# One attention and expert kernel: its projections issued as pairs of 64-column matmuls right behind P V, half of its score peaks copied out of PSUM by ScalarE, and its expert items in another order

## The chip, the cores and the metric

One core of one Trainium2 chip. The metric is the device time of one launch in microseconds (us), the median of several runs. The inputs are fixed, everything is float32.

## What is computed

A transformer block with adaptive layer norm, batch 1, 2048 tokens of width 128:

```python
mod = (silu(c) @ wmod)              # six vectors of 128: shift, scale, gate, twice
h = layernorm(x) * (1 + ca) + sa
x = x + ga * attention(h)           # 16 heads of 64
h = layernorm(x) * (1 + cb) + sb
x = x + gb * experts(h)             # 8 experts of 128, top 2 by sigmoid, and one shared expert
```

The attention reads its projections with a plain `reshape(1, 16, 2048, 64)` of the (2048, 1024) result. So head n uses tokens 128n to 128n+127 alone, and each of these tokens gives 16 "positions" of 64 values: 2048 positions per head. The scores are 2048 x 2048 per head, followed by softmax and P V. The expert part multiplies each token by the router's weight before and after an expert's SwiGLU, and sums over the chosen two; the shared expert has no weight.

## The kernel before

**Work.** The kernel goes through 16 heads; a head is two units (half 0 and half 1 of its queries), a unit is 16 key tiles (kt), and two key tiles are a step, so a unit has 8 steps and 32 places, numbered 4 x step + 0 to 3. On TensorE (PE) places 0 and 1 of a step are the scores of one key tile each (`scores`, L1149 to L1179), places 2 and 3 the product of probabilities and values of one key tile of the step before (`weigh`, L1182 to L1194). Scores are split into three products of float32r parts (hi x hi, hi x lo, lo x hi: L1166, L1169, L1172), each a pair of matmuls in two row tiles of the array (64 rows by 128 columns). `weigh` (L1190) is float32 in two column tiles (128 rows by 64 columns, `tile_position=(0, 0)` and `(0, 64)`).

**Peaks.** The softmax needs the largest score of each query ahead of time. A pair (`pair`, L1099 to L1115) is a rough product of 128 queries with 512 keys in each of two PSUM banks (6 and 7). VectorE (DVE) reduces it to its maximum (`pair`, L918 to L929, the reduction is L924). There are 16 pairs per unit, for the next unit or the one after. PE issues one at each place 1 and one at each place 3, and each waits until the banks of the one before are free (`peak_free`). After pair 15 the partial maxima are reduced to 8 per query (L928), PE transposes them (`turn_shift`, L1122), DVE keeps them and a DMA spreads them for the next unit's scores (L1178).

**Side jobs.** `side_jobs` (L80) lays out by hand at which place each job of a unit is issued: `LONG_JOBS` has the projections of the next head (q twice, k twice, v twice: `side`, L1082 to L1097), the output projection of the head before (`project`, L1207 to L1216) and the shift. `SUM_PLACES` has the sums over the probabilities (`sum_unit`, L1203), `SCALE_PLACES` the reciprocals in four parts (L944) and the scaling (L951), `LOW_PLACES` the low parts of q and k (L901, L907, L915). All these jobs go through PSUM bank 5 and wait for `job_free`. Within a place the order is that of the list: pairs first, then the long jobs. Every engine walks the same plan in its own program, so a job's place sets the order of work on PE, DVE, ScalarE (ACT) and on SP's DMA queue.

**Other engines.** ACT takes the exponentials, 128 x 1024 per key tile (L786), copies q, k and v out of PSUM (`side`, L705 to L715; k twice, L710 and L712), rounds the step of k (L720) and copies P V (L737). GpSimd (POOL) sums the probabilities, 15 adds of 128 x 1024 per unit (`add_tile`, L851). PE's sum of a unit waits for all 15 of them.

**Experts.** 36 items: 4 groups of 512 tokens, in each the shared expert and then the 8 experts (`ORDER`, L392). An item is two up products (L439, L440), SiLU on ACT (L481), products on DVE (L546, L548) and four down products (L425). The routed items need their tokens weighted first (`weigh_tokens`, L408, L413): items 1 and 2 (`FIRST_WEIGHED`) on DVE, all others on POOL, behind its last attention add. `SUM_AFTER` and the names beside it (L403 to L406) say behind which item the rest of the last head's work comes: its sum needs POOL's last add.

Of the kernel before, what the change touches and what calls it, by code (L numbers as in the profile page):

```python
# [11 lines left out]
P = 128  # L12
# [6 lines left out]
BANK = 512  # L19
# [31 lines left out]
    {6: ("inv", 0), 7: ("inv", 1), 9: ("inv", 2), 11: ("inv", 3), 13: ("scale", 0)},  # L51
    {10: ("inv", 0), 12: ("inv", 1), 15: ("inv", 2), 19: ("inv", 3), 21: ("scale", 0)},
# [27 lines left out]
def side_jobs(half, sums=True, project=True, pairs=True, early=True, last_head=False):  # L80

    places = [[] for _ in range(4 * PAIRS)]
    if sums:
        places[SUM_PLACES[half]].append(("sum", 0))
# [7 lines left out]
    for place, (kind, i) in LONG_JOBS[half].items():  # L92
        if sums if kind == "out" else pairs if kind == "shift" else project:
            places[place].append((kind, i))
# [12 lines left out]
def build(nc, x, wq, wk, wv, wo, gate_w, w1, w2, w3, sw1, sw2, sw3, expert_bias, cond, wmod, out):  # L107
    with ExitStack() as ctx:
# [53 lines left out]
        mod_t = sb("mod_t", [P, 4, 2])  # L162
        peak_parts = sb("peak_parts", [P, 2, PEAK_PAIRS // STRETCHES, STRETCHES])
        peak = sb("peak", [P, 8])
# [35 lines left out]
        peak_full, peak_free = sem("peak_full"), sem("peak_free")  # L200
        tail_full, tail_free = sem("tail_full"), sem("tail_free")
# [27 lines left out]
        class Tail:  # L229

            def __init__(self, n):
                self.n, self.full = n, n + 1
                self.bank = PEAK_BANK + n % 2 if n < TAIL_PAIRED else PV_BANK
                self.earlier = n - 1 if n < TAIL_PAIRED else n
                self.ps = ps[:, self.bank, :]

# [155 lines left out]
        ORDER = [EXPERTS] + list(range(EXPERTS))  # L392

        def routed(m):

            return m // ALL * EXPERTS + m % ALL - 1

        ITEMS = GROUPS * ALL

        FIRST_WEIGHED = (1, 2)  # L400
# [4 lines left out]
        GATE_AFTER = (13, 14, 15, 16)  # L405
        LATE_AFTER = {10: ("turn", 3), 12: ("logits", 1), 18: ("weights", 3)}  # L406

        def weigh_tokens(eng, m, signal):  # L408
            g, e = m // ALL, ORDER[m % ALL]
            eng.wait_ge(weights_loaded[e], 16 * (g + 1))  # L410
            if m >= 3:
                eng.wait_ge(ups, m - 1)
# [3 lines left out]
        def ffn_pe(pe, tail_job, sum_last, project_last):  # L416
            def down(m):
                g, e = m // ALL, ORDER[m % ALL]
                if m == 0:
                    pe.wait_ge(tail_free, TAIL_PAIRED)  # L420
                if m % ALL == 0 and g >= 2:
                    pe.wait_ge(out_ready, g - 1)
                pe.wait_ge(inner_w_ready, m + 1)
                for k in range(4):
                    mm = pe.matmul(ps[:, 6 + g % 2, k * P:(k + 1) * P], inner_w[m % 2][:, k * P:(k + 1) * P],  # L425
                                   w2T[:, e, :], start=(m % ALL == 0 and k == 0),
                                   stop=(m % ALL == ALL - 1 and k == 3), skip_group_check=True)
                mm.then_inc(downs, 1)

            for m in range(ITEMS):  # L430
                g, e = m // ALL, ORDER[m % ALL]
                rhs = hT[:, g * BANK:(g + 1) * BANK] if e == EXPERTS else weighted[m % 2]
                if m in FIRST_WEIGHED:
                    pe.wait_ge(weighted_first, m)
# [86 lines left out]
        def ffn_dve(dve, link, invert, scale_outputs, add_head):  # L521
            def add_up(g):

                dve.wait_ge(downs, ALL * (g + 1))
# [6 lines left out]
            for m in FIRST_WEIGHED:  # L531
# [4 lines left out]
            for m in range(ITEMS):  # L536
                g, e = m // ALL, ORDER[m % ALL]
# [7 lines left out]
                else:  # L545
                    dve.tensor_tensor(inner[m % 2], silu_sb[m % 2], banks(m)[1], ALU.mult).then_inc(inner_ready, 1)  # L546
                    dve.wait_ge(inner_ready, m + 1)
                    dve.tensor_tensor(inner_w[m % 2], inner[m % 2], token_weight[e], ALU.mult).then_inc(inner_w_ready, 1)  # L548
                if m in INVERT_AFTER:
# [14 lines left out]
                if m % ALL == 1 and g > 0:  # L564
                    add_up(g - 1)
            add_up(GROUPS - 1)

        def spread_weights(sp, g):
# [3 lines left out]
            for e in range(EXPERTS):  # L572
                if g > 0:

                    sp.wait_ge(inner_w_ready, (g - 1) * ALL + ORDER.index(e) + 1)
# [92 lines left out]
        def _(act):  # L668
# [59 lines left out]


# [37 lines left out]
            def body(t):  # L767
                local = 0
                for p, half, head, unit, plan in units(t):
# [4 lines left out]
                    for step, places in enumerate(plan):  # L774
                        for place, jobs in enumerate(places):
# [13 lines left out]
                            for kind, i in jobs:  # L789
                                if kind in COUNTED:  # L790
                                    side(Job(jobs_at(t) + local), kind, i, 1 - p)
                                if kind == "step k":
                                    round_step(Job(jobs_at(t) + (local - 1)), i, 1 - p, head * 2 + (3 + i))
# [520 lines left out]
```

## Time and profile before

| | us |
|---|---|
| median of 3 runs | 1387.61 |
| lowest and highest | 1387.3, 1387.88 |
| profiled execution, its own time | 1388.47 |
| its span | 1386.7 |
| granted TensorE clock over the span | 0.992 of full speed |
| busy: PE, POOL, DVE, ACT | 1361.5, 1186.4, 908.4, 663.7 |

The span runs from the first to the last instruction of the profiled execution; 1.8 us of its time lie around it. Its own time is 0.9 us above the median of the runs. In the timelines a line merges instructions of one kind: its start, the time from there to the end of the last, how many they are, and in brackets the idle time before it. PE stands for matmuls, PEld for weight loads. A matmul whose weights were not loaded ahead is recorded from the start of that load.

### The profile page before, as it was taken

The numbers are of one execution on the slowest core, as the hardware profiler recorded it, in microseconds if no ns is written. First come the engines' busy times: TensorE is split into PE (matmuls) and PEld (weight loads), VectorE is DVE, ScalarE is ACT, GpSimd is POOL, SyncE is SP. The second block draws the span as 40 slices with busy tenths as digits, with TensorE's granted clock in tenths as the row PEclk, the third lists the DMA queues.
The fourth block names the chain that finished last, engine by engine and source line by source line (L and its number), as shares of the span: only waits on it lengthen the run. The fifth ranks groups of instructions, "written<-read, shape, count | busy, mean of one in ns | idle before, by whom it ended". The sixth has DMA issues, their size and how long they took to land.

```text
span 1386.7 us, 19883 instructions
## 1 busy us (share of the span) xinstructions
PE 1361.5 (98%) x7850; PEld 697.3 (50%) x7850; DVE 908.4 (66%) x1023; ACT 663.7 (48%) x837; POOL 1186.4 (86%) x537
## 2 busy tenths in 40 slices
PE   7999999999999999999999999999999999999898
PEld 5444545454554545454454545454545545454565
DVE  6767666676767676676767676666767676746554
ACT  6444444444544445444544445445445444464331
POOL 2499999898989899999989898998989898989443
PEclk9999999999999999999999999999999999999999
DMA  7010201020100202020200102020201001003231
GB/s 199 8 40 1 46 2 46 2 47 0 33 15 2 46 1 47 1 47 1 46 1 20 28 1 47 1 47 1 46 1 37 11 2 45 1 1 69 60 96 53
DMA packets 31950, 41.39 MB, mean 30 GB/s; under 512 B 4298, under 2 KB 15186, under 8 KB 31858
## 3 DMA queue, kind: packets, MB, share of 16 engines
q1 hardware_dynamic: 31714, 40.13, 12.1%
q8 instruction: 62, 1.02, 0.3%
q14 instruction: 30, 0.25, 0.1%
q10 hardware_dynamic: 144, 0.00, 0.0%
HBM read 13.70 MB, written 1.11 MB: 11 GB/s over the span
## 4 chain that ended last, share of the span: by engine, by line
PE 93%; POOL 3%; DVE 2%; ACT 1%; issue 0%; DMA 0%; SPq 0%; POOLq 0%; DVEq 0%
PE ps L1190 33%; PE ps L1114 14%; PE ps L1166 10%; PE ps L1172 8%; PE ps L1169 8%; PE ps L1093 5%; POOL acc L851 2%; PE ps L1096 2%; PE ps L1214 2%; PE ps L425 2%; PE ps L439 2%; PE ps L440 2%; PE ps L1203 2%; DVE peak_parts L924 1%; PE ps L1178 1%
## 5 line engine op out<-in xcount | busy, mean ns | idle before, releaser
L851 POOL TENSOR_TENSOR acc<-acc,probs 128x1024 f32<-128x1024 f32 x448 | 1066.6, 2381 | 92.6 <-ACT probs L786 32.1
L924 DVE TENSOR_REDUCE peak_parts<-ps 128x2 f32<-128x1024 f32 x512 | 621.7, 1216 | 312.7 <-PE ps L1114 311.0
L786 ACT ACTIVATE probs<-ps 128x1024 f32<-128x1024 f32 x512 | 502.5, 1029 | 394.6 <-PE ps L1172 326.2
L1190 PE MATMUL ps<-probs,v_sb 128*64 128x512 f32 x2048 | 501.2, 605 | 0.0
L1190 PEld LDWEIGHTS ps<-probs,v_sb 128*64 128x64 f32 x2048 | 124.3, 136 | 222.4 <-issue 168.0
L1166 PE MATMUL ps<-q_hi,d_hi 64*128 64x512 f32 x512 | 213.0, 416 | 0.0
L1166 PE MATMUL ps<-q_hi,d_swap_hi 64*128 64x512 f32 x512 | 212.9, 416 | 0.0
L1172 PE MATMUL ps<-q_hi,d_lo 64*128 64x512 f32 x512 | 200.5, 392 | 0.0
L1169 PE MATMUL ps<-q_lo,d_swap_hi 64*128 64x512 f32 x512 | 200.4, 391 | 0.0
L1169 PE MATMUL ps<-q_lo,d_hi 64*128 64x512 f32 x512 | 200.3, 391 | 0.0
L1172 PE MATMUL ps<-q_hi,d_swap_lo 64*128 64x512 f32 x512 | 200.3, 391 | 0.0
L944 DVE RECIPROCAL ps<-ps 128x128 f32<-128x128 f32 x128 | 121.8, 955 | 18.8 <-PE ps L1203 18.8
L1114 PE MATMUL ps<-k_hi,q_hi 64*128 64x512 f32 x512 | 121.8, 472 | 5.1 <-DVE peak_parts L924 2.6
L1114 PE MATMUL ps<-k_swap_hi,q_hi 64*128 64x512 f32 x512 | 120.9, 469 | 2.2 <-DVE peak_parts L924 2.0
L1114 PEld LDWEIGHTS ps<-k_hi,q_hi 64*128 64x128 f32 x512 | 47.9, 183 | 132.4 <-DVE peak_parts L924 114.0
L1166 PEld LDWEIGHTS ps<-q_hi,d_hi 64*128 64x128 f32 x512 | 94.9, 185 | 36.3 <-issue 24.9
L1114 PEld LDWEIGHTS ps<-k_swap_hi,q_hi 64*128 64x128 f32 x512 | 48.1, 184 | 125.9 <-DVE peak_parts L924 109.9
L1172 PEld LDWEIGHTS ps<-q_hi,d_swap_lo 64*128 64x128 f32 x512 | 94.9, 185 | 11.8
L1166 PEld LDWEIGHTS ps<-q_hi,d_swap_hi 64*128 64x128 f32 x512 | 94.9, 185 | 11.7
L1172 PEld LDWEIGHTS ps<-q_hi,d_lo 64*128 64x128 f32 x512 | 94.9, 185 | 11.0
L1169 PEld LDWEIGHTS ps<-q_lo,d_swap_hi 64*128 64x128 f32 x512 | 95.1, 186 | 9.7
L1169 PEld LDWEIGHTS ps<-q_lo,d_hi 64*128 64x128 f32 x512 | 95.2, 186 | 8.0
(146 smaller groups left out, 1062.4 us busy)
## 6 DMA issues: line engine op xcount, KB each, us to landing
k_swap_hi<-k_hi SPq DMA_DIRECT2D x64, 128.0 KB, 2.3
d_swap_hi<-d_hi SPq DMA_DIRECT2D x64, 128.0 KB, 2.3
d_swap_lo<-d_lo SPq DMA_DIRECT2D x64, 128.0 KB, 2.3
token_weights<-weights_dram SPq DMA_DIRECT2D x32, 256.0 KB, 3.3
probs<-in_L_ffn_w_dram SPq DMA_DIRECT2D x2, 512.0 KB, 5.9
shifts<-shift_sb SPq DMA_DIRECT2D x64, 2.0 KB
out_dram<-probs SPq DMA_DIRECT2D x4, 256.0 KB, 3.1
x_in<-in_L_attn_x_dram SPq DMA_DIRECT2D x1, 960.0 KB, 8.8
```

The lines of the kernel that those rows point to most:

```text
L425: mm = pe.matmul(ps[:, 6 + g % 2, k * P:(k + 1) * P], inner_w[m % 2][:, k * P:(k + 1) * P], w2T[:, e, :], start=(m % ALL == 0 and k == 0), ...
L439: pe.matmul(banks(m)[0], w1T[:, e, :], rhs, start=True, stop=True)
L786: act.activation(probs[:, kt % PROBS, :], ps[:, 2 * place:2 * place + 2, :].rearrange("p a b -> p (a b)"), ACT.Exp, scale=SCALE).then_inc( ...
L851: pool.tensor_tensor(total, total if kt > 1 else probs[:, 0, :], probs[:, kt % PROBS, :], ALU.add).then_inc(added, 1)
L924: dve.tensor_reduce(peak_parts[:, :, i // STRETCHES, i % STRETCHES], ps[:, bank:bank + 2, :], AX.X, ALU.max).then_inc(peak_free, 1)
L944: dve.reciprocal(job.ps[:, cols], job.ps[:, cols]).then_inc(part_inverted, 1)
L1093: mm = pe.matmul(job.ps[:, k * P:(k + 1) * P], w[:, at:at + P], h_head[:, :], start=True, stop=True)
L1114: mm = pe.matmul(ps[:, bank + b, :], q_hi[at, target_parity, q:q + P], keys[at, target_parity, cols], start=True, stop=True, tile_position ...
L1166: pe.matmul(ps[:, slot + b, :], hi[b][at[b], p, cols], q_hi[at[b], p, q], start=kt < 2, stop=False, tile_position=(b * HEAD_DIM, 0), skip_ ...
L1169: pe.matmul(ps[:, slot + b, :], hi[b][at[b], p, cols], q_lo[at[b], p, q], start=False, stop=False, tile_position=(b * HEAD_DIM, 0), skip_g ...
L1172: mm = pe.matmul(ps[:, slot + b, :], lo[b][at[b], p, cols], q_hi[at[b], p, q], start=False, stop=kt >= 2, tile_position=(b * HEAD_DIM, 0), ...
L1190: mm = pe.matmul(ps[at:at + HEAD_DIM, PV_BANK, :], v_sb[:, p, chunk_of(kt) * HEAD_DIM:(chunk_of(kt) + 1) * HEAD_DIM], probs[:, kt % PROBS, ...
```

## The change

1. The long jobs come ahead of the pair in their place, the shift moves from place 25 to 26 and `out` from 27 to 23; both now follow a `weigh`. All of q, k, v, `out` and the shift are written as column tiles of 64, as `weigh` is.
2. ACT copies every odd pair (both banks, 128 x 1024) to a new SBUF buffer `peak_copy` (`take_pair`) and frees the banks. DVE reduces the copy (`taken`), one odd place later, behind the even pair that is issued there; pairs 15 and 3 are reduced in their own place. ACT's next copy waits until DVE has read the one before (`copy_read`).
3. The low parts of k and most of the reciprocals move by one to three places.
4. The expert items: the shared items of groups 1, 2 and 3 each move ahead of the routed items of the group before (the last ahead of group 2), the items weighted by DVE are three, and the work of the last head comes one item later.

```diff
 LONG_JOBS = (
-    {3: ("q", 0), 15: ("k", 0), 19: ("k", 1), 25: ("shift", 0), 27: ("out", 0)},
-    {3: ("q", 1), 7: ("v", 0), 25: ("shift", 0), 27: ("v", 1)},
+    {3: ("q", 0), 6: ("sum", 0), 15: ("k", 0), 19: ("k", 1), 23: ("out", 0), 26: ("shift", 0)},
+    {3: ("q", 1), 7: ("v", 0), 10: ("sum", 0), 26: ("shift", 0), 27: ("v", 1)},
 )
-SUM_PLACES = (6, 10)
 LOW_PLACES = (
-    {4: ("low q", 0), 16: ("step k", 0), 18: ("low k", 0), 20: ("step k", 1), 22: ("low k", 1)},
+    {4: ("low q", 0), 15: ("step k", 0), 16: ("low k", 0), 19: ("step k", 1), 20: ("low k", 1)},
     {4: ("low q", 1)},
 )
 SCALE_PLACES = (
-    {6: ("inv", 0), 7: ("inv", 1), 9: ("inv", 2), 11: ("inv", 3), 13: ("scale", 0)},
-    {10: ("inv", 0), 12: ("inv", 1), 15: ("inv", 2), 19: ("inv", 3), 21: ("scale", 0)},
+    {6: ("inv", 0), 8: ("inv", 1), 9: ("inv", 2), 11: ("inv", 3), 12: ("scale", 0)},
+    {10: ("inv", 0), 12: ("inv", 1), 14: ("inv", 2), 17: ("inv", 3), 19: ("scale", 0)},
 )
...
+    for i in range(1, PEAK_PAIRS, 2):
+        place = 2 * ((i - EARLY_PAIRS) % PEAK_PAIRS) + 1
+        if pairs if i >= EARLY_PAIRS else early:
+            places[place if i == PEAK_PAIRS - 1 or place + 2 > 4 * PAIRS else place + 2].append(("taken", i))
...
-        ORDER = [EXPERTS] + list(range(EXPERTS))
+        SEQUENCE = [(0, EXPERTS), (1, EXPERTS)] + [(0, e) for e in range(EXPERTS)] \
+            + [(2, EXPERTS)] + [(1, e) for e in range(EXPERTS)] + [(3, EXPERTS)] \
+            + [(g, e) for g in (2, 3) for e in range(EXPERTS)]
...
+        FIRST_WEIGHED = ROUTED[:3]
-        SUM_AFTER, INVERT_AFTER, SCALE_AFTER, PROJECT_AFTER, ADD_AFTER = 3, (3, 4), 5, 6, 6
-        STATS_AFTER, ROOT_AFTER, RSTD_AFTER, NORM_AFTER = 7, 8, 8, 9
+        SUM_AFTER, INVERT_AFTER, SCALE_AFTER, PROJECT_AFTER, ADD_AFTER = 4, (4, 5), 6, 7, 7
+        STATS_AFTER, ROOT_AFTER, RSTD_AFTER, NORM_AFTER = 8, 9, 9, 10
...
+            def take_pair(i, pairs_earlier, target_unit):
+                act.wait_ge(peak_full, pairs_earlier + 1)
+                act.wait_ge(copy_read, copies(target_unit, i))
+                act.copy(peak_copy[:, :, :], ps[:, PEAK_BANK:PEAK_BANK + 2, :]).then_inc(peak_free, 1)
...
+            def taken(i, pairs_earlier, copies_earlier):
+                dve.wait_ge(peak_free, pairs_earlier + 1)
+                dve.tensor_reduce(peak_parts[:, :, i // STRETCHES, i % STRETCHES], peak_copy[:, :, :], AX.X,
+                                  ALU.max).then_inc(copy_read, 1)
...
                     for k in range(4):
-                        at = i * BANK + k * P
-                        mm = pe.matmul(job.ps[:, k * P:(k + 1) * P], w[:, at:at + P], h_head[:, :],
-                                       start=True, stop=True)
+                        for at in (0, HEAD_DIM):
+                            col = i * BANK + k * P + at
+                            mm = pe.matmul(job.ps[at:at + HEAD_DIM, k * P:(k + 1) * P], w[:, col:col + HEAD_DIM],
+                                           h_head[:, :], start=True, stop=True, tile_position=(0, at))
...
-                pe.transpose(job.ps[0:8, 0:P], peak[:, :], ident[:, :]).then_inc(job_full, 1)
+                pe.matmul(job.ps[0:HEAD_DIM, 0:P], peak[:, :], ident[:, :], start=True, stop=True,
+                          tile_position=(0, 0)).then_inc(job_full, 1)
```

`v` and `project` are split in the same way as q and k. `peak` grows from 8 to 64 columns, cleared once by POOL at the start. The prologue, which works out the first unit's peaks, keeps its reductions on DVE alone.

## Rows read from the trace of the kernel before

**Rows 1.** The page: busy us, share and instructions of each engine
```profile
PE 1361.5 (98%) x7850; PEld 697.3 (50%) x7850; DVE 908.4 (66%) x1023; ACT 663.7 (48%) x837; POOL 1186.4 (86%) x537
```
**Rows 2.** The chain that ended last, its longest pieces: start, us, what
```profile
155.00 1.98 PE ps L1214 x16
...
1155.62 1.98 PE ps L1214 x16
...
1246.77 3.06 POOL acc L851
```
**Rows 3.** Timeline of PE, an ordinary step (pair to pair to pair)
```profile
411.27 0.50 PE L1114 MATMUL ps<-k_swap_hi,q_hi 64*128 64x512 f32 x2
...
412.78 0.39 PE L1172 MATMUL ps<-q_hi,d_swap_lo 64*128 64x512 f32 x1
...
413.10 0.50 PE L1114 MATMUL ps<-k_hi,q_hi 64*128 64x512 f32 x2
413.52 1.94 PE L1190 MATMUL ps<-probs,v_sb 128*64 128x512 f32 x8
415.39 0.50 PE L1114 MATMUL ps<-k_hi,q_hi 64*128 64x512 f32 x2
```
**Rows 4.** Timeline of DVE in that step
```profile
411.82 1.23 DVE L924 TENSOR_REDUCE peak_parts<-ps 128x2 f32<-128x1024 f32 x1 [0.96 <-PE ps L1114]
...
412.96 0.95 DVE L944 RECIPROCAL ps<-ps 128x128 f32<-128x128 f32 x1
```
**Rows 5.** Timeline of PE, a step whose even pair did not wait
```profile
426.58 0.39 PE L1172 MATMUL ps<-q_hi,d_lo 64*128 64x512 f32 x1
426.81 0.39 PE L1114 MATMUL ps<-k_swap_hi,q_hi 64*128 64x512 f32 x2
427.13 1.94 PE L1190 MATMUL ps<-probs,v_sb 128*64 128x512 f32 x8
```
**Rows 6.** Groups by line: busy us, mean ns of one, idle before
```profile
L1114 PE MATMUL ps<-k_hi,q_hi 64*128 64x512 f32 x512 | 121.8, 472 | 5.1 <-DVE peak_parts L924 2.6 <-DVE d_lo L915 2.4
```
**Rows 7.** Timeline of PE around one q job
```profile
433.37 0.50 PE L1114 MATMUL ps<-k_hi,q_hi 64*128 64x512 f32 x2
433.80 1.16 PE L1093 MATMUL ps<-h_head,wqT 128*128 128x128 f32 x8
...
436.15 0.39 PE L1172 MATMUL ps<-q_hi,d_lo 64*128 64x512 f32 x1
```
**Rows 8.** Timeline of ACT behind one k job
```profile
449.29 0.59 ACT L710 CAST k_hi<-ps 128x512 fp32r<-128x512 f32 x1 [2.57 <-PE ps L1093]
...
450.25 1.05 ACT L786 ACTIVATE probs<-ps 128x1024 f32<-128x1024 f32 x1
```
**Rows 9.** Timeline of POOL over one head (two units)
```profile
395.38 2.35 POOL L851 TENSOR_TENSOR acc<-probs 128x1024 f32<-128x1024 f32 x1
399.62 4.89 POOL L851 TENSOR_TENSOR acc<-acc,probs 128x1024 f32<-128x1024 f32 x2 [1.88 <-ACT probs L786]
...
472.33 2.35 POOL L851 TENSOR_TENSOR acc<-probs 128x1024 f32<-128x1024 f32 x1
```
**Rows 10.** Timeline of PE over the first expert items
```profile
1274.07 1.13 PE L439 MATMUL ps<-hT,w1T 128*128 128x512 f32 x2
...
1286.11 2.07 PE L439 MATMUL ps<-acc,w1T 128*128 128x512 f32 x2 [4.66 <-POOL acc L413]
...
1308.35 1.02 PE L439 MATMUL ps<-hT,w1T 128*128 128x512 f32 x2
...
1310.96 1.02 PE L439 MATMUL ps<-acc,w1T 128*128 128x512 f32 x2
```
**Rows 11.** Busy us by stretch: us, PE, PEld, DVE, ACT, POOL, granted clock
```profile
1286.00:1292.70 6.70, 6.59 (x16) 2.44 (x17) 2.11 (x3) 0.60 (x1) 2.55 (x3) 0.57 0.01 2
```
**Rows 12.** Timeline of DVE at the router's work
```profile
1247.62 3.01 DVE L512 TENSOR_TENSOR wkT<-wkT,earlier 128x768 f32<-128x768 f32 x1
...
1253.71 0.95 DVE L516 TENSOR_REDUCE wvT<-wqT 128x96 f32<-128x768 f32 x1
```

More of the change, by code:

```diff
@@ L82, in side_jobs @@
     places = [[] for _ in range(4 * PAIRS)]
-    if sums:
-        places[SUM_PLACES[half]].append(("sum", 0))
+    for place, (kind, i) in LONG_JOBS[half].items():
+        if sums if kind in ("sum", "out") else pairs if kind == "shift" else project:
+            places[place].append((kind, i))
     if pairs:
@@ L162, in build @@
         mod_t = sb("mod_t", [P, 4, 2])
+        peak_copy = sb("peak_copy", [P, 2, BANK])
         peak_parts = sb("peak_parts", [P, 2, PEAK_PAIRS // STRETCHES, STRETCHES])
-        peak = sb("peak", [P, 8])
+        peak = sb("peak", [P, HEAD_DIM])
         shift_sb = sb("shift_sb", [8, 2, P], F32R)
@@ L235, in __init__, with copies @@
                 self.ps = ps[:, self.bank, :]
+        def copies(target_unit, i):
+            return (i - EARLY_PAIRS) // 2 if target_unit == 1 else (
+                (PEAK_PAIRS - EARLY_PAIRS) // 2 + (target_unit - 2) * (PEAK_PAIRS // 2) + i // 2)
         def adds(kt):
@@ L793, in body @@
                                     round_step(Job(jobs_at(t) + (local - 1)), i, 1 - p, head * 2 + (3 + i))
+                                if kind == "pair" and i % 2 == 1:
+                                    target = unit + (1 if i >= EARLY_PAIRS else 2)
+                                    take_pair(i, target * PEAK_PAIRS + i, target)
                                 if kind == "sum":
@@ L812, in _ @@
         def _(pool):
+            pool.memset(peak[:, :], 0.0)
             pool.memset(ident[:, :], 0.0).then_inc(consts, 1)
@@ L860, in _ @@
             for m in range(ITEMS):
-                if m not in FIRST_WEIGHED and ORDER[m % ALL] < EXPERTS:
+                if m not in FIRST_WEIGHED and SEQUENCE[m][1] < EXPERTS:
                     weigh_tokens(pool, m, weighted_ready)
@@ L988, in body @@
                                 job = Job(jobs_at(t) + local)
-                                if kind == "pair":
+                                if kind == "pair" and i % 2 == 0:
                                     target = unit + (1 if i >= EARLY_PAIRS else 2)
                                     pair(i, target * PEAK_PAIRS + i, target, PEAK_BANK)
+                                if kind == "taken":
+                                    target = unit + (1 if i >= EARLY_PAIRS else 2)
+                                    taken(i, target * PEAK_PAIRS + i, copies(target, i))
                                 if kind == "low q":
@@ L1213, in project @@
                     for k in range(4):
-                        mm = pe.matmul(job.ps[:, 0:DIM], oT[:, half, k * P:(k + 1) * P], wo2[:, 4 * half + k, :],
-                                       start=(half == 0 and k == 0), stop=(half == 1 and k == 3))
+                        for at in (0, HEAD_DIM):
+                            col = k * P + at
+                            mm = pe.matmul(job.ps[at:at + HEAD_DIM, 0:DIM], oT[:, half, col:col + HEAD_DIM],
+                                           wo2[:, 4 * half + k, :], start=(half == 0 and k == 0),
+                                           stop=(half == 1 and k == 3), tile_position=(0, at))
                 mm.then_inc(out_full, 1)
```

59 lines of the change are left out of this document (34 added, 25 removed).

## The prediction

> **What bounds it now.** I read the busy shares first, then the chain, then PE's timeline of one ordinary step, then POOL's of one head. PE is busy 98% of the span, POOL 86% [rows 1], but a busy share of PE hides weight loads that nothing covers. The chain is PE nearly throughout. It passes the output projection (L1214) at 155.00 and 1155.62 us, 13 heads apart: **76.97 us per head** [rows 2]. Only in the last unit does it cross to POOL's adds.
>
> In an ordinary step [rows 3] PE goes from odd pair (411.27) to scores, even pair (413.10), P V (413.52) and the next odd pair (415.39): 4.12 us. From the last scores to the even pair it takes 0.32 and from there to P V 0.42. Where nothing holds the pair these are 0.23 and 0.32 [rows 5], so the wait costs 0.19 to 0.20. DVE is what it waits for: its reduction of the odd pair starts 0.55 after that pair and takes 1.23, up to 413.05 [rows 4], and PE wanted the banks by 412.9. A held pair also exposes its weight load: its record is 0.50 long instead of 0.39. The mean of 0.472 over all pairs [rows 6] makes 0.08/0.11, some 74%, of them exposed; odd pairs, half of all, always are, because they follow another array mode. So 0.48 of the 256 even pairs wait: some 123 x 0.2 = 24 us, **1.5 us per head**.
>
> POOL sets a floor close below [rows 9]. Its first add of a unit pair starts at 395.38 and again at 472.33, 76.95 later, and in between it waits once for an exponential, 1.88 us where some 0.14 passes between any two adds. All else is adds end to end: 75.1 to 75.2 us per head. **No head can get shorter by more than 1.8 us** while the adds stay as they are.
>
> **Jobs as column tiles.** A q job now costs 2.78 - 1.51 = 1.27 us: pair to last scores is 433.37 to 436.15 with it [rows 7] and 411.27 to 412.78 without [rows 3]. Eight half-products take 0.9 of that; the rest is leaving and entering the row mode. Behind P V and in its mode it needs no switch of its own, if two 64-column tiles run side by side as in P V, whose eight records make four pairs of 0.43 in 1.87 with both mode changes. Then q and k cost 8 x 0.11 = 0.9, v 0.86, the output projection 1.8, each some 0.38 less than before. Seven per head: 2.7 us. The shift goes from 0.3 to 0.2, twice: 0.2 more. Sum **2.9 us per head**. Bounds of this term: 0 where the short tiles cost an extra 0.4 per job, 2.9 where all is as in P V, and below zero in the rival of that name; I take 2.9, since P V is the nearest row in form.
>
> **ACT's copy.** A copy of 128 x 1024 is not in the trace; the exponential of that size from PSUM takes 1.05 [rows 8]. It starts 0.55 after the odd pair, as DVE did, and ends 0.18 us sooner than DVE's 1.23. With 0.05 for the semaphore the next weight load starts 1.63 after the odd pair and PE wants its matmul at 1.72: alone, this ends nearly all of the wait. But `peak_copy` is one buffer, and DVE reads it behind the even pair. The loop is: even pair lands 0.44 after its start, DVE's reduction 1.14 (start to start, 411.82 to 412.96 [rows 4]), its second reduction some 1.2 (from SBUF 768 columns took 0.95 [rows 12], so 1024 about 1.2), 0.05, copy 1.05, 0.05, load 0.11: 4.04 us, against 3.91 for PE's own step (4.12 less the wait). So an ordinary step still stalls 0.1, less where a job gives slack. Bounds per ordinary step: 0 and the old 0.2.
>
> Where ACT has other work first it is late. For q and v one copy of 0.48 (two start to start in 0.96 [rows 8]) fits into the 0.55; almost nothing. For k there are two, and now they come just ahead of the pair: ACT begins them 0.1 after the odd pair's start, is free at 1.06, the copy ends at 2.1, and the pair wanted at 1.72 runs at about 2.25: **0.53 per k, 1.1 per head**. DVE's step of k then waits for ACT and ACT's rounding for DVE, in order, but exponentials have a step of slack. Pairs 15 and 3 are reduced in their own place: DVE is held until ACT's copy, `peak_ready` comes some 0.2 late for the shift, and v at place 27 waits some 0.4 for `job_free` behind DVE's copy of the shift: 0.8 per head. The walk through 16 steps gives, with some 0.8 for ordinary steps, **2.7 us of stalls per head** where there are 1.5 now.
>
> The reciprocals only fill DVE: two plus two reductions are 4.2 us in a step of 4.8 with the sum's 0.86. Nothing moves on SP's queue but the swaps of k's low part, two places earlier, and the shift's DMA, one later; both land within a step. POOL's program in the loop is untouched.
>
> **Per head**: 2.9 + 1.5 - 2.7 = 1.7, and POOL's floor is 1.8. I take **1.7 x 15 = 25.5 us**. The last head has no projections, and ACT's norms and table loads (1.3 us each way) now stand ahead of copies that free PE's banks: +2 us, an estimate from those durations. The memset of `peak` lies under the first loads; it would cost 0.2 without them.
>
> **Experts.** Item 3 starts at 1286.11, after 4.66 us of idle PE: its tokens are weighted on POOL behind the last add. Item 9 starts at 1308.35, 34.3 us after item 0 [rows 10]. Its steady pace is 2.61 (1308.35 to 1310.96), so nine items, the sum (0.9) and the projection (1.8), less the down product that comes after item 9, are 25.3: 9 us are lost, part of it because the clock fell behind the idle time, to a mean of 0.57 over 6.7 us [rows 11], which is mostly the level of 1.2 GHz. The new order puts two more items, 5.2 us of work, ahead of POOL's first product. DVE's third weighting (2.7 us beside POOL) leaves a gap of 1.5. I find item 9 at 27.2 instead of 34.3: **7 us less**; bounds 3 (the clock falls all the same) and 9.
>
> **Sum** against the profiled execution: 1386.7 - 25.5 + 2 - 7 = 1356.2 of span, 1.8 around it. The median of the runs lies 0.9 above the span, so 1357.
>
> **Rivals.**
> - *The copies hold PE.* Ordinary steps keep their old 0.2 and k costs 0.8: stalls of 3.9 per head, 0.5 saved: 1387.6 - 7.5 + 2 - 7 = 1375. For it: the loop of 4.04 has no spare, and every wait on three engines adds its 0.05. Against it: the same rows, since reductions overlap by 0.1. 0.22 for this and what lies between.
> - *Short column tiles don't overlap* (slower). L1093 has 16 records per job where there were 8 at 0.11 each [rows 7], the output projection 32. At one record per 0.11 they cost 0.9 more per q and k and 1.8 more per projection: 5.4 per head. Less 1.7, times 15, less 5 in the rest: 1387.6 + 55 - 5 = 1438. It decides from a pace at which two such tiles cost 0.04 more than one. Against it: in P V two tiles start together. But no stretch of the trace has records as dense as one per 0.055. 0.07.
> - *DVE's reading of SBUF holds POOL* (slower). Beside a product of two SBUF operands on DVE (3.01 for 768 columns [rows 12]) POOL's add took 3.06 [rows 2] instead of the usual 2.38. It decides from 0.06 us on the mean add, which is all of POOL's 1.8 per head; 0.68 on 8 of 15 adds is 5.4 per unit, 4.5 more than POOL has free: 1387.6 + 32 x 4.5 - 5 = 1527. Against it: the SBUF reduction behind it took only 0.95 [rows 12] with POOL at work. 0.03.
> - *The change does little.* Stalls eat what the modes give, the experts' 7 us stay hidden behind the group's weights: within 3 us. 0.04.
>
> The Trainium skill, "TensorE: Matmul & The Clock Gate", section "Wait — 56ns, not 53.3ns?", speaks against the short tiles: without hardware decode the sequencer needs about 62 ns per matmul and becomes the bound where the array's work is shorter. By that a q job would take 16 x 62 = 0.99 us and the projection 1.98, an estimate of 0.55 us more per head and 1365 in the end. No row here shows a matmul held by its issue.
>
> **Numbers.** Forecast 0.6 (1349 to 1362 on its own), copies 0.22, tiles 0.07, contention 0.03, little 0.04, something better than POOL's floor 0.04. A measurement of this kernel tells about 0.2%, 2.8 us. Faster by more 0.87, within 0.04, slower 0.09. The range leaves out the slower two: from POOL's floor with 9 us in the experts (1387.6 - 27 - 9 = 1351, less 3 for a last head without its penalty, 1348) to the held copies and a little beyond, 1378.
>
> **What would show it.** The distance of two L1214 in the chain: 75.2 to 75.4. POOL without its 1.9 us wait. L1114's mean nearer to 0.45. q, k at 0.9 with records in twos, and a row-to-column change only once per step each way. The even pair behind each k released by ACT, some 0.5 late. Item 9 some 27 us behind item 0 at full clock. Wrong if L1093 comes in single records at 0.11, if L851's mean rises over 2.4, or if even pairs wait for ACT by over 0.2 in most steps.

## The result, and the profile after

| | before | after |
|---|---|---|
| median of the runs, us | 1387.74 | **1365.74** |
| lowest and highest | 1387.3, 1388.03 | 1365.35, 1368.03 |
| ratio to before, 95% interval | | 0.9845 [0.9828, 0.9862] |
| span of the profiled execution | 1386.7 | 1364.0 |

The change is faster by 22 us, where 30.6 were forecast. The time lies in the range of 1348 to 1378, 9 us above the forecast and above the 1349 to 1362 that the forecast gave itself: between it and the rival *The copies hold PE*. The page of the kernel after gives for the engines (busy us, share, instructions):

```profile
PE 1326.9 (97%) x8714; PEld 693.8 (51%) x8714; DVE 900.8 (66%) x1024; ACT 886.2 (65%) x1083; POOL 1189.5 (87%) x537
```

PE is less busy by 35 us [rows 1], and the span is shorter by 23: the rest has become waiting. The first and the 14th output projection on PE's timeline (start, us, engine, line, operation, operands, count) give the length of a head:

```profile
149.03 1.59 PE L1262 MATMUL ps<-wo,oT 128*64 128x128 f32 x26
...
1131.78 1.59 PE L1262 MATMUL ps<-wo,oT 128*64 128x128 f32 x26
```

982.75 / 13 = **75.60 us per head**, 1.37 less than before [rows 2]. What a job costs now, and what happens behind a k, stands in the same timeline:

```profile
451.29 1.92 PE L1262 MATMUL ps<-wo,oT 128*64 128x128 f32 x32
453.13 0.50 PE L1159 MATMUL ps<-k_swap_hi,q_hi 64*128 64x512 f32 x2
...
463.97 1.94 PE L1236 MATMUL ps<-probs,v_sb 128*64 128x512 f32 x8
465.74 1.04 PE L1136 MATMUL ps<-h_head,wqT 128*64 128x128 f32 x16
466.71 0.51 PE L1159 MATMUL ps<-k_hi,q_hi 64*128 64x512 f32 x2
...
522.73 0.49 PE L1159 MATMUL ps<-k_hi,q_hi 64*128 64x512 f32 x2
...
524.23 0.39 PE L1218 MATMUL ps<-q_hi,d_lo 64*128 64x512 f32 x1
524.90 0.50 PE L1159 MATMUL ps<-k_swap_hi,q_hi 64*128 64x512 f32 x2 [0.28 <-ACT peak_copy L752]
525.33 1.94 PE L1236 MATMUL ps<-probs,v_sb 128*64 128x512 f32 x8
```

From P V to the job 1.77, from there to the pair 0.97; without a job P V to pair takes 1.87 [rows 3]. The q job thus adds 0.87, where it added 1.27 before [rows 7]. The projection adds 1.74. Sixteen records of q lie in 1.04, eight pairs at 0.11, the two of a pair 0.007 apart: the short tiles do run in twos. That term was right. Behind k the last scores to the even pair take 0.67 and the pair to P V 0.43, instead of 0.23 and 0.32: 0.55 for each k. ACT shows why:

```profile
522.85 0.59 ACT L729 CAST k_hi<-ps 128x512 fp32r<-128x512 f32 x1 [1.00 <-PE ps L1136]
523.33 0.59 ACT L731 COPY k_raw<-ps 128x512 f32<-128x512 f32 x1
523.81 1.03 ACT L752 COPY peak_copy<-ps 128x1024 f32<-128x1024 f32 x1
```

The two copies of k stand ahead of the copy that frees the banks, as forecast. In the other steps little is left to wait for: the median even pair starts 0.23 behind the last scores, and only its weights come a little late (0.39 to P V instead of 0.32). The waits by line of the whole stretch from 300 to 1200 us (us in total, times, longest), 12 heads, name the other places:

```profile
ACT peak_copy L752 <- DVE peak_parts L963: 90.2, 73, 3.0
...
PEld ps L1159 <- DVE peak_parts L953: 71.6, 86, 2.1
...
PEld ps L1159 <- ACT peak_copy L752: 46.3, 153, 0.8
...
PEld ps L1140 <- DVE shift_sb L975: 12.5, 12, 1.0
...
POOL acc L880 <- ACT probs L811: 3.1, 9, 0.4
```

73 times ACT could not copy because DVE had not read the copy before, and v waits once per head for the shift. POOL, which before had a pause of 1.9 us in every head, has almost none.

In the experts item 9 starts 29.14 us behind item 0, before 34.28 [rows 10], and the granted clock from 1250 to 1300 us is 1.00 (the last column but two):

```profile
1255.61 1.12 PE L456 MATMUL ps<-hT,w1T 128*128 128x512 f32 x2
...
1267.72 1.13 PE L456 MATMUL ps<-acc,w1T 128*128 128x512 f32 x2 [1.59 <-DVE acc L430]
...
1284.75 1.02 PE L456 MATMUL ps<-acc,w1T 128*128 128x512 f32 x2
```
```profile
1250.00:1300.00 50.00, 46.99 (x241) 27.34 (x237) 30.18 (x45) 18.28 (x27) 29.37 (x17) 1.00 0.33 80
```

From item 0 to the end of the span there are 108.4 us, before 112.6: 4.2 less. Up to item 0 there are 18.5 less. That is the whole difference of 22.7.

### The profile page after: what moved, and what is told of

Its sections match the earlier page's. It is cut to its first block, busy times and chain, and to the rows that moved or that the text cites. A ratio compares the mean times of both kernels' runs of the same rounds, so it can differ in the third digit from the quotient of the medians.

```text
span 1364.0 us, 22091 instructions
## 1 busy us (share of the span) xinstructions
PE 1326.9 (97%) x8714; PEld 693.8 (51%) x8714; DVE 900.8 (66%) x1024; ACT 886.2 (65%) x1083; POOL 1189.5 (87%) x537
## 3 DMA queue, kind: packets, MB, share of 16 engines
q8 instruction: 69, 1.13, 0.4%
## 4 chain that ended last, share of the span: by engine, by line
PE 83%; DVE 8%; ACT 6%; issue 3%; DMA 0%; SPq 0%; DVEq 0%; ACTq 0%
PE ps L1236 30%; PE ps L1159 12%; PE ps L1212 7%; PE ps L1218 7%; PE ps L1215 7%; PE ps L1136 4%; ACT peak_copy L752 3%; DVE peak_parts L963 3%; DVE peak_parts L953 3%; PE ps L1140 2%; PE ps L1262 2%; PE ps L456 2%; PE ps L442 2%; PE ps L1249 2%; PE ps L457 2%
## 5 line engine op out<-in xcount | busy, mean ns | idle before, releaser
L880 POOL TENSOR_TENSOR acc<-acc,probs 128x1024 f32<-128x1024 f32 x448 | 1069.5, 2387 | 71.6 <-ACT probs L811 7.8
L1236 PE MATMUL ps<-probs,v_sb 128*64 128x512 f32 x2048 | 513.0, 606 | 0.0
L953 DVE TENSOR_REDUCE peak_parts<-ps 128x2 f32<-128x1024 f32 x266 | 324.2, 1223 | 195.4 <-PE ps L1159 190.6
L752 ACT COPY peak_copy<-ps 128x1024 f32<-128x1024 f32 x246 | 250.8, 1019 | 224.4 <-DVE peak_parts L963 115.5
L963 DVE TENSOR_REDUCE peak_parts<-peak_copy 128x2 f32<-128x1024 f32 x246 | 298.5, 1213 | 70.3 <-ACT peak_copy L752 70.3
L1212 PE MATMUL ps<-q_hi,d_hi 64*128 64x512 f32 x512 | 201.6, 394 | 1.2 <-ACT probs L811 1.2
L1212 PE MATMUL ps<-q_hi,d_swap_hi 64*128 64x512 f32 x512 | 201.6, 394 | 0.0
L983 DVE RECIPROCAL ps<-ps 128x128 f32<-128x128 f32 x128 | 115.2, 935 | 0.0
L880 POOL TENSOR_TENSOR acc<-probs 128x1024 f32<-128x1024 f32 x32 | 76.2, 2380 | 27.4 <-ACT probs L811 27.4
```

Source lines behind the costliest of these rows:

```text
L752: act.copy(peak_copy[:, :, :], ps[:, PEAK_BANK:PEAK_BANK + 2, :]).then_inc(peak_free, 1)
L880: pool.tensor_tensor(total, total if kt > 1 else probs[:, 0, :], probs[:, kt % PROBS, :], ALU.add).then_inc(added, 1)
L953: dve.tensor_reduce(peak_parts[:, :, i // STRETCHES, i % STRETCHES], ps[:, bank:bank + 2, :], AX.X, ALU.max).then_inc(peak_free, 1)
L963: dve.tensor_reduce(peak_parts[:, :, i // STRETCHES, i % STRETCHES], peak_copy[:, :, :], AX.X, ALU.max).then_inc(copy_read, 1)
L983: dve.reciprocal(job.ps[:, cols], job.ps[:, cols]).then_inc(part_inverted, 1)
L1212: pe.matmul(ps[:, slot + b, :], hi[b][at[b], p, cols], q_hi[at[b], p, q], start=kt < 2, stop=False, tile_position=(b * HEAD_DIM, 0), skip_ ...
```

## The experiments

Each ran beside the kernel before on one chip; its time is the median, and "less" or "more" is against the kernel before in the same runs. The length of a head is always that of the first to the 14th projection.

### One part at a time

**modes_alone**: column tiles and places, without ScalarE's copies and with the old order of experts. From the kernel after:

```diff
-SEQUENCE = [(0, EXPERTS), (1, EXPERTS)] + [(0, e) for e in range(EXPERTS)] + ...
+SEQUENCE = [(g, e) for g in range(GROUPS) for e in [EXPERTS] + list(range(EXPERTS))]
-FIRST_WEIGHED = ROUTED[:3]
+FIRST_WEIGHED = ROUTED[:2]
...                                                    # SUM_AFTER and its kin, as before
-places[...].append(("taken", i))
-if kind == "pair" and i % 2 == 1: take_pair(...)      # ScalarE
-if kind == "pair" and i % 2 == 0: pair(...)           # VectorE
+if kind == "pair": pair(...)
```

> The kernel before with the jobs moved behind P V and cut into column tiles, their DVE steps at the new places, and nothing else: no copy on ScalarE, the old order of experts. Theory: the tiles save some 3 us per head, the waits of the even pairs for DVE stay at 1.5 or rise to 2.2, and POOL's adds allow no head under 75.2 us, so a head takes 75.2 to 76.0 instead of 76.97 and the whole 1361 to 1375 us. Rival (the copies are what makes the gain possible, the modes alone are given back as longer waits for DVE): a head of 76.5 us or more, 1380 us or more.

1368.64 us, ratio 0.9866 [0.9852, 0.9879]: 18.9 us less. On PE's timeline:

```profile
148.54 1.70 PE L1254 MATMUL ps<-wo,oT 128*64 128x128 f32 x28
...
1130.65 1.70 PE L1254 MATMUL ps<-wo,oT 128*64 128x128 f32 x28
```

75.55 us per head, the same as with the copies. **The copies bring nothing to a head of the kernel after.** Here every ordinary even pair waits for DVE, as the step shows that begins at 480.31 (0.33 to the pair, 0.43 to P V):

```profile
481.80 0.39 PE L1210 MATMUL ps<-q_hi,d_lo 64*128 64x512 f32 x1
482.13 0.50 PE L1151 MATMUL ps<-k_hi,q_hi 64*128 64x512 f32 x2
482.56 1.94 PE L1228 MATMUL ps<-probs,v_sb 128*64 128x512 f32 x8
```

The pairs' mean duration is 0.498 and 0.484 us in its two groups, so by the reckoning of the prediction some 85% of the even pairs wait: 16 x 0.85 x 0.2 = 2.7 us per head, where before they were 1.5. Counted pair by pair on PE's timelines from 300 to 1185 us (what they take beyond 0.22 from the last scores and 0.32 to P V), 87% of them wait 0.21 here, 3.0 us per head; in the kernel before 35% do, 1.3 us per head. Shorter jobs left DVE less time, and the old wait grew. The prediction had set the copies' stalls against the 1.5 of before; they should have been set against these 3.0.

**copy_alone**: ScalarE's copies on the kernel before (its jobs, places and order of experts kept); `take_pair`, `taken` and their dispatch as in the change.

> The kernel before with ScalarE copying every second pair of peaks and DVE reducing the copy, and nothing else. ScalarE takes the pair ahead of the copies of k here, since the pair stands first in a place. Theory: waits of the ordinary steps go from 0.2 to 0.1 us, no loss behind k, some loss at the shift and in the last head: 0.3 to 0.9 us per head less, 1375 to 1384 us. Rival (the new loop over three engines costs as much as it frees, or DVE's reading of SBUF slows POOL): 1386 us or more.

1438.54 us, ratio 1.0368 [1.0354, 1.0382]: 51 us more, 80.19 us per head. The time lies in the open range of the rival (1386 us or more), but neither theory had such a loss or its place. The waits of that kernel, from 300 to 1200 us:

```profile
PE ps L1156 <- DVE peak L959: 24.6, 23, 1.1
...
PEld ps L1127 <- DVE d_lo L936: 12.7, 12, 1.1
PEld ps L1127 <- DVE oT L982: 12.7, 12, 1.1
```

The shift (L1156), in place 25, comes right behind the last reduction, and that reduction is now a copy and a read: 1.07 us of idle PE, twice per head, and the weights of two of the q and k jobs (L1127) wait 1.1, their matmuls 0.7, for DVE steps that stand behind reductions of copies. From pair to pair the shift costs 1.13 more than before (3.63 instead of 2.50), twice per head, and these two jobs 0.8 each: 3.9 lost. The even pairs' waits did fall, from 1.3 to 0.6 us per head, as the first theory had it; 3.9 less 0.7 is the 3.2 measured. In the kernel after, where the shift stands in place 26 and the steps of k in the place of the job, the shift costs only 0.2 more than in modes_alone (2.70 instead of 2.51). So the new places seem to be what makes the copies bearable; they were not tried by themselves, and here ScalarE also takes the pair ahead of the copies of k. What the copies cost depends on what DVE has to end next, not on their own 1.02 us.

**experts_alone**: the new SEQUENCE, its helpers and three first weightings on VectorE, on the kernel before.

> The kernel before with the new order of the experts' items and three first weightings on DVE, and nothing else. Theory: item 9 comes 5 us sooner behind item 0 and about 1 us is lost again behind it, as in the kernel after: 4 us less, 1382.5 to 1384.5 us, and TensorE's clock in the stage is granted in full. Rival (part of what the stage saves in the kernel after comes from POOL ending its adds closer to PE): 2 us less or under, 1385.5 us or more.

1384.69 us, ratio 0.9978 [0.997, 0.9987]: 2.9 us less, with 1.8 to 4.2 in the interval; just above the 1382.5 to 1384.5 of the theory and under the 1385.5 of the rival. In the profiled executions the stage from item 0 to the end takes 108.0 us instead of 112.6 and the whole 4.3 less. The order is worth 3 to 4 us, with the attention as it was.

So modes_alone and experts_alone add up to 21.8 us, and the whole change gives 22.0.

**wide_tiles**: the kernel after with 128-column products.

```diff
-for at in (0, HEAD_DIM):
-    mm = pe.matmul(job.ps[at:at + HEAD_DIM, ...], w[:, col:col + HEAD_DIM], h_head[:, :], ..., tile_position=(0, at))
+mm = pe.matmul(job.ps[:, k * P:(k + 1) * P], w[:, at:at + P], h_head[:, :], start=True, stop=True)
```

> The kernel after, but q, k, v and the output projection as 128-column products again, at the new places. Theory: the saving is in the two column tiles that run in the mode of P V; without them each of seven jobs per head pays for leaving and entering that mode, 0.38 us each, 2.7 us per head: 1400 to 1408 us. Rival (the new places and the other order of jobs make the gain, the form of the tiles little): 1367 to 1375 us.

1384.20 us, ratio 0.9977 [0.9967, 0.9986]; 76.87 us per head. Between the two theories: the tiles are worth 1.27 us per head, not 2.7. Its timeline around a k job:

```profile
449.68 1.94 PE L1233 MATMUL ps<-probs,v_sb 128*64 128x512 f32 x8
451.55 1.16 PE L1135 MATMUL ps<-h_head,wkT 128*128 128x128 f32 x8
452.64 0.50 PE L1156 MATMUL ps<-k_hi,q_hi 64*128 64x512 f32 x2
```

1.87 and 1.09, where the column tiles take 1.77 and 0.97: 0.22 per job, of which a head has seven. One of them, the v that waits for the shift's copy, takes 4.05 instead of 4.00 from pair to pair and so gains only 0.05; with the other six that makes some 1.4, close to the 1.27 measured. The rest of the 0.4 that a job saves comes from its place alone. An explanation that fits both, though no run tries it by itself: between P V and the pair the array changes its mode anyway, so a full-width job there adds one change, and between pair and scores, where it was, two, at some 0.2 each.

**modes_experts**: the kernel after without the copies, all else kept.

> The kernel after without ScalarE's copies: VectorE reduces all pairs from PSUM, all else as in the kernel after. Theory: heads of 75.5 as in modes_alone, no loss of 2.5 us in the last head, and the experts' 3 to 4 us: 1362.5 to 1365.5 us, at or under the kernel after. Rival (the copies free VectorE for something that modes_alone didn't show): 1368 us or more.

**1363.45 us**, ratio 0.9824 [0.9809, 0.9838], 75.53 us per head: the simpler kernel is as fast as the one with the copies, and in the medians 2.3 us faster (the two intervals overlap). That gain is not where the expectation had it. Item 0 starts at 1254.67, only 0.94 sooner, and the stage behind it takes 106.5 us instead of 108.4. The third weighting on DVE shows the reason for the 1.9, first in the kernel after, then in modes_experts:

```profile
1264.84 2.83 DVE L430 TENSOR_TENSOR acc<-hT,token_weights 128x512 f32<-128x512 f32 x1
```
```profile
1263.98 0.68 DVE L430 TENSOR_TENSOR acc<-hT,token_weights 128x512 f32<-128x512 f32 x1
```

POOL's last adds (start, us to the end of the last), again first in the kernel after, then in modes_experts:

```profile
1259.51 7.61 POOL L880 TENSOR_TENSOR acc<-acc,probs 128x1024 f32<-128x1024 f32 x3
```
```profile
1256.15 7.35 POOL L877 TENSOR_TENSOR acc<-acc,probs 128x1024 f32<-128x1024 f32 x3
```

In the kernel after POOL is still adding, up to 1267.1, and the same product takes four times as long; there PE waits 1.59 us for it. In modes_experts POOL's adds are done at 1263.5, and its next product starts only after DVE's has begun. The kernels with three weightings on DVE and the new places fall into two kinds: 2.83 or 2.84 for the product and 107.6 to 108.8 us for the stage (the kernel after, wide_tiles, and below two_copies and where_free_two), or 0.68 to 0.69 and 106.0 to 106.6 us (modes_experts, and below taken_first, after_narrow, copies_where_free and where_free_two_narrow). experts_alone, with the old places, lies between in the product (1.75) and has a stage of 108.0.

POOL ends 3.6 us later in the kernel after. Of these, 1.9 have built up over the heads before (its first add of the last head starts at 1185.64 instead of 1183.71), and 1.7 come in the last head, which stalls: there the norms stand ahead of DVE's read and ACT's copy, and on PE's timeline

```profile
1197.36 0.50 PE L1159 MATMUL ps<-k_swap_hi,q_hi 64*128 64x512 f32 x2 [1.25 <-DVE peak_parts L953]
...
1206.88 0.50 PE L1159 MATMUL ps<-k_swap_hi,q_hi 64*128 64x512 f32 x2 [1.45 <-ACT peak_copy L752]
```

PE starts item 0 only 0.94 later all the same; POOL, whose adds have nothing to spare, stays behind.

### Is it the copies' order, their buffer, or POOL?

**taken_first**: the kernel after, but ScalarE's dispatch of a place begins with the pair.

```diff
-for kind, i in jobs:
+taking = [job for job in jobs if job[0] == "pair" and job[1] % 2 == 1]
+for kind, i in taking + [job for job in jobs if job not in taking]:
```

> The kernel after, but where ScalarE has a pair to copy and a job's copy in the same place, it copies the pair first. Theory: the 0.53 us that each even pair behind a k waits for ScalarE goes, 1.1 us per head; GpSimd's adds let at most 0.3 to 0.4 of it through: a head of 75.2, 1359 to 1362 us. Rival (the steps of k then come late and hold VectorE's next reductions, and the wait moves): 1364 us or more.

1402.22 us, ratio 1.0103 [1.0088, 1.0118], 77.76 us per head: 2.2 worse than the kernel after. The rival, and larger than it was put:

```profile
PEld ps L1263 <- DVE d_lo L945: 18.8, 12, 1.6
PEld ps L1137 <- DVE d_lo L945: 18.6, 12, 1.6
...
PE ps L1237 <- ACT o_raw L762: 10.5, 23, 0.5
```

There is one bank for all jobs, freed by the last step of k. That step comes later by a copy and two semaphores, and the next k job (L1137) and the projection (L1263) each wait 1.6 us with their weights. Their matmuls start 0.85 later than in the kernel after (1.27 behind the last record of P V instead of 0.42), and P V waits 0.5 twice per head for ACT's copy of the one before: 2.6 lost. Gained is about 0.55, since only one of the two even pairs behind a k no longer starts late. Putting k first was the cheaper evil.

**after_narrow** and **modes_narrow**: GpSimd adds 960 of 1024 columns, from the second add of a unit on; the sums of 64 columns are left out.

```diff
-pool.tensor_tensor(total, total if kt > 1 else probs[:, 0, :], probs[:, kt % PROBS, :], ALU.add)
+w = slice(0, 960 if kt > 1 else 1024)
+pool.tensor_tensor(total[:, w], total[:, w] if kt > 1 else probs[:, 0, w], probs[:, kt % PROBS, w], ALU.add)
```

> The kernel after, with all but the first of GpSimd's 15 adds of a unit cut from 1024 to 960 columns (the sums of 64 columns are left out), so that GpSimd has some 4 us more to spare in every head. Theory: GpSimd's own work, 75.2 us per head, lies 0.3 under the 75.58 that a head takes, and TensorE waits for the copies: the head stays at 75.4 to 75.6 and the whole at 1363 to 1366 us. Rival (the adds set the end after all, through the exponentials that wait for their slots): the head falls under 75.2, the whole under 1360 us.

> The kernel of modes_alone (column tiles and places, no copies, old order of experts) with the same cut of GpSimd's adds. modes_alone took 75.54 us per head and the kernel after, with the copies, 75.58. Theory 1 (two different chains happen to give the same): TensorE's path with all pairs reduced on VectorE is 75.5 by itself, so the cut changes nothing, 1367 to 1369.5 us. Theory 2 (both kernels run against GpSimd's adds, and that is why the copies bring nothing): the head falls by 0.3 us or more, to 1364 us or less.

1365.46 us (0.9841 [0.9826, 0.9856]) and 1368.02 us (0.9858 [0.9842, 0.9875]): unchanged both, 75.57 and 75.53 us per head. The adds got shorter, and POOL only waits more, in after_narrow:

```profile
L881 POOL TENSOR_TENSOR acc<-acc,probs 128x960 f32<-128x960 f32 x448 | 1007.5, 2249 | 129.6 <-ACT probs L811 73.4 <-POOL acc L881 1.8
```

(2249 ns each instead of 2387, idle before them 129.6 us instead of 71.6.) So POOL bounds neither kernel. That both take 75.5 looks like chance: TensorE's path has two different sums of waits, 3.0 per head at the even pairs in modes_alone, and in the kernel after 2.1 there and 0.8 at the shift and v.

**two_copies**: two buffers for the copies.

```diff
-peak_copy = sb("peak_copy", [P, 2, BANK])
+peak_copy = token_weights[:, 0:4, :].rearrange("p (n b) j -> p n b j", n=2)
-act.wait_ge(copy_read, copies(target_unit, i))
+act.wait_ge(copy_read, copies(target_unit, i) - 1)     # none for the first copy
```

> The kernel after with two buffers for the copied peaks instead of one, so that ScalarE copies the next pair while VectorE still reads the last. Theory: in an ordinary step the even pair waits 0.1 us because the copy waits for VectorE's read of the one before; with two buffers this goes, some 1.1 to 1.4 us per head, of which GpSimd's own 75.2 us per head let 0.3 to 0.4 through: 1359 to 1362 us. Rival (the copy is late for another reason: ScalarE's other work, or VectorE, whose reductions take the same time in all): 1364.5 us or more.

1363.10 us, ratio 0.983 [0.9813, 0.9847], 75.41 us per head: 0.2 of the 0.3 to 0.4 that POOL would let through. The even pairs' waits fell by 0.6 per head (from 2.1 to 1.5), so the second buffer does what it should, and most of it is not let through. In the medians it is above the forecast by 1 us and 2.6 below the kernel after; the intervals overlap.

**copies_where_free** and **where_free_two**: ScalarE copies fewer pairs, with one buffer and with two.

```diff
+def copied(half, i, last_head):
+    if last_head or i % 2 == 0 or i in (3, PEAK_PAIRS - 1):
+        return False
+    return not (half == 0 and i in (11, 13))
-if kind == "pair" and i % 2 == 1: take_pair(...)       # ScalarE
+if kind == "pair" and copied(half, i, last_head): take_pair(...)
```

> The kernel after, one buffer, but ScalarE copies a pair only where nothing else stands in its way: not in the two places where it has k to copy, not the pair behind which the peaks are complete nor the one that is reduced in its own place, and none in the last head; VectorE reduces those from PSUM. Theory: behind k the even pair waits 0.2 instead of 0.54 us, the shift and v come in time, the last head has no loss: with the ordinary steps' 0.13 that is 74.6 us per head on TensorE, over which GpSimd's 75.2 to 75.3 then stands: 1358 to 1361 us. Rival (a mixed order has the worse of both, each single copy starting the same loop): 1363 us or more, no better than no copies at all (1363.45).

> copies_where_free with two buffers. Theory: if copies_where_free already stands at GpSimd's 75.2 to 75.3 us per head, the second buffer adds nothing, within 1 us of it; if it is above, this one comes to 75.2 to 75.3 and 1358 to 1360 us. Rival (ScalarE's copies without VectorE's pacing come ahead of exponentials that then start late): slower than copies_where_free by 2 us or more.

1364.62 (0.9834 [0.9819, 0.9849]) and 1364.88 us (0.9837 [0.9822, 0.9852]): no better than no copies, by the time alone the rival of the first. The second buffer changes nothing, as expected. But the heads are 75.38 in both, 0.15 under modes_experts, and the end gives that back. In where_free_two it takes 126.5 us from the 14th projection to item 0 instead of 124.0, and the third weighting collides again (2.84 us). In copies_where_free PE idles once for 4.9 us, for DVE's work on the router. Why these waits arise was not looked into.

In where_free_two PE's sum over the probabilities, which needs all of POOL's adds, waits for them once per head; in the kernel after that wait does not occur (from 300 to 1200 us: us in total, times, longest):

```profile
PE ps L1265 <- POOL acc L893: 16.6, 12, 2.0
```

POOL runs end to end, over the stretch of [rows 9]:

```profile
391.28 2.37 POOL L893 TENSOR_TENSOR acc<-probs 128x1024 f32<-128x1024 f32 x1
393.79 32.69 POOL L893 TENSOR_TENSOR acc<-acc,probs 128x1024 f32<-128x1024 f32 x13
426.91 2.35 POOL L893 TENSOR_TENSOR acc<-acc,probs 128x1024 f32<-128x1024 f32 x1 [0.43 <-POOL acc L893]
429.23 2.34 POOL L893 TENSOR_TENSOR acc<-probs 128x1024 f32<-128x1024 f32 x1
431.71 35.18 POOL L893 TENSOR_TENSOR acc<-acc,probs 128x1024 f32<-128x1024 f32 x14
466.85 2.37 POOL L893 TENSOR_TENSOR acc<-probs 128x1024 f32<-128x1024 f32 x1
```

75.57 from one first add to the one a head later, without a wait for an exponential. Whether TensorE's path lies below is the last question.

**where_free_two_narrow**: where_free_two with GpSimd's adds cut as above (64 columns of the sums left out).

> where_free_two (copies only where ScalarE is free, two buffers) with all but the first of GpSimd's adds of a unit cut to 960 columns, as in after_narrow. In after_narrow the cut left the head where it was, since TensorE set it. Theory: in where_free_two, with heads of 75.2 to 75.6, GpSimd's adds are the bound, and with 4 us to spare TensorE's own path shows: 74.3 to 74.9 us per head, 1345 to 1356 us. Rival (TensorE's path is near 75.3 by itself, and the copies can't bring more): heads of 75.1 or more, 1360 us or more.

**1336.83 us**, ratio 0.9635 [0.9619, 0.9651], 28 us less than where_free_two:

```profile
146.77 1.81 PE L1279 MATMUL ps<-wo,oT 128*64 128x128 f32 x30
...
1106.43 1.81 PE L1279 MATMUL ps<-wo,oT 128*64 128x128 f32 x30
```

73.82 us per head. The theory, and 8 us below its range: the same cut that gave nothing in the kernel after gives 1.6 us per head here, and PE's wait for POOL's adds is gone. Well placed, the copies are worth 1.7 us of TensorE's path per head (75.53 in modes_narrow, where the adds are cut too, to 73.82), and GpSimd takes 1.6 of it. A step whose odd pair is copied now has no wait left, 0.22 and 0.32, as in [rows 5]:

```profile
468.62 0.39 PE L1235 MATMUL ps<-q_hi,d_swap_lo 64*128 64x512 f32 x1
468.84 0.39 PE L1176 MATMUL ps<-k_swap_hi,q_hi 64*128 64x512 f32 x2
469.16 1.94 PE L1253 MATMUL ps<-probs,v_sb 128*64 128x512 f32 x8
```

How GpSimd could be given less to add without leaving sums out was not tried.

## Why the prediction was right, and where it was off

The forecast was faster by 30.6 us, the measurement 22, inside the range. In the spans, where the prediction made its sum:

| term | predicted | measured |
|---|---|---|
| 15 heads | 25.5 | 20.6 (15 x 1.37) |
| last head | -2 | -2.1 (the remainder, since item 0 is 18.5 sooner) |
| experts | 7 | 4.2 |
| sum | 30.5 | 22.7 |

- *Jobs as column tiles*: right. 0.87 for q where 0.9 stood, 1.74 for the projection where 1.8 stood; two tiles per 0.11 us, never one. The division was not seen: 0.22 of a job's 0.4 is the tile, the rest its new place (wide_tiles). The slower rival of short tiles that don't overlap is refuted by the record spacing.
- *Stalls of the copies, 2.7 per head*: mis-sized, but by little, and so were the waits of before. Counted as above, the even pairs wait 1.3 per head in the kernel before, where the prediction reckoned 1.5 from the pairs' mean, and 2.1 in the kernel after: 1.1 behind k, as forecast, and 1.0 in ordinary steps, where 0.8 stood. The shift and v add 0.8, as forecast (2.70 and 4.00 us from pair to pair, against 2.51 and 3.37 in modes_alone). That is 2.9 where 2.7 stood, and with some 3.0 for the jobs 3.0 + 1.3 - 2.9 = 1.4 per head, 1.37 by the projections. So two slips of 0.2 in the same direction, less the 0.1 that the jobs gave, make the 1.7 too high by 0.3. *The copies hold PE* had put 3.9, so the truth lies nearer to the forecast.
- *What the copies are worth*: here the reasoning, not a number, had a hole. "Before's stalls 1.5" was credited to the copies. But 1.5 (counted, 1.3) is what DVE's wait costs beside the old, longer jobs; beside the short ones it costs 3.0 (modes_alone), just what the copies cost. The forecast was near in total and credited the wrong part, which is luck as far as the copies go.
- *POOL's floor, 75.1 to 75.2*: the floor is real (where_free_two against where_free_two_narrow). It lies near 75.4 as PE and POOL meet, a little above the forecast, and the kernel after, at 75.60, does not stand on it (after_narrow). "No head can get shorter by more than 1.8 us" held; nothing came lower than 1.6 below the kernel before until the adds were cut.
- *DVE's reading of SBUF holds POOL*: wrong, as forecast. The add's mean went from 2381 to 2387 ns, where the rival needed 0.06 us.
- *Last head*: right in sum. Part of its stall reaches the end by a way that the prediction did not have, POOL's lateness and the third weighting.
- *Experts, 7*: mis-sized. Item 9 came 5.1 sooner instead of 7, and 0.9 of that was lost again. The wait for DVE's third weighting was there (1.59, forecast 1.5), and the granted clock stayed at 1.00, the level of 2.4 GHz. Not forecast were the projection's 0.67 behind the scaled outputs, the down products' 0.4 and 0.8 behind DVE, and that the third weighting would fall together with POOL's last add by a matter of 3 us: where it does not, item 9 comes at 27.4 (modes_experts; 27.2 was forecast).
- *The signs*: POOL's pause is gone, q and k come in twos, the even pair behind k is released by ACT 0.5 late, and none of the three "wrong if" occurred. A head of 75.2 to 75.4 (75.60), a pair's mean nearer to 0.45 (0.472 and 0.476) and item 9 at 27 (29.1) did not come. In the chances, the parts that are faster add up to 0.86 and the slower ones to 0.10, where 0.87 and 0.09 stood.
- *The sequencer's time per matmul*: the Trainium skill, "TensorE: Matmul & The Clock Gate", section "Wait — 56ns, not 53.3ns?", has the sequencer take 62 ns per matmul where hardware decode is off, which would make 0.99 us for a q job and 1.98 for the projection. Measured are 0.87 and 1.74, with 16 records in 8 steps of 0.109, so 0.055 each. The total of 1365 that this would give matches the median by accident; the mechanism is not seen here.

## What to carry to other kernels

When a change shortens work that stood beside a wait, price the wait again as it will be without that cover, and give each part only what it saves over the version without it: two parts that look like one gain can be one gain and one exchange of waits. A copy that frees a bank earlier is worth its place only where neither the copying engine nor the reader has something more urgent in front or behind. And cut an engine's work artificially before and after a mend: the same cut gave nothing, then 28 us.

## What the runs showed of the hardware that was not expected

- Column tiles of 64 by 128 run in twos at the pace of one 128-column product of the same moving width: 0.109 us for the two against 0.112.
- A job that changes the array's mode costs 0.22 us more than one in the mode of its forerunner (1.87 + 1.09 against 1.77 + 0.97). It starts 0.10 later, its second record comes 0.10 later (0.21 behind the first instead of 0.11), and only 0.02 is the pace. The Trainium skill, "TensorEngine Tiling (Array Packing)", section "Key Properties", states that a change of tiling mode drains the engine; the trace agrees, with these 0.2 us.
- A product of two SBUF operands of 128x512 takes 0.68 us on VectorE when no GpSimd instruction is under way at its start and 2.83 when one of GpSimd's adds is, whose own time grows only from 2.36 to 2.61. A reduction of 128x1024 from SBUF takes 1.213 beside the same adds, against 1.223 from PSUM, and the add's mean stays at 2.387: it is the product with two SBUF operands that collides with GpSimd, not every reading of SBUF. The Trainium skill, "SBUF — State Buffer", section "SBUF: two separate sides", states that a VectorE operation with two SBUF inputs and a GpSimd operation that reads SBUF exclude each other for a whole instruction. The trace agrees: 2.83 is 0.68 and most of one add.
